# Two recurrent layers of a fused model: output copies on ScalarE, adds to X and one weighting on GpSimd

## The reference, cut to what matters

```
v = x @ value_w.T ;  r = sigmoid(x @ recep_w.T)
wkv_t = (e1_t * aa_t + e2_t * v_t) / (e1_t * bb_t + e2_t + 1e-6)
aa_{t+1} = e1b_t * aa_t + e2b_t * v_t
return (r * wkv) @ out_w.T
```

```
multiplier = sqrt(max(1 - a*a, 1e-7)) ;  normed_x = x * gate_x * multiplier
p_prefix = max(shifted cumprod(a), 1e-7)
S = cumsum(normed_x / p_prefix) ;  h = p_prefix * S ;  return h
```

## Time and profile before

| | us |
|---|---|
| median of 3 runs | 3088.95 |
| lowest and highest run | 3085.35 and 3089.32 |
| the profiled execution | 3088.85 |
| its span, first to last instruction | 3087.0 |
| window of the first recurrent loop, 207.5 to 252.4 | 44.90 |
| window of the second layer's last loop, 1893 to 1926.6 | 33.60 |

### The profile page before, as it was taken

The page is one execution under the profiler, slowest core; times in us unless marked ns, Lnnn a source line. Parts: engine busy times, 40 slices in busy tenths (PEclk is TensorE's granted clock), DMA queues, the critical chain, the costliest instruction groups (busy, mean ns, idle before and its releaser), DMA issues. The chain is left out here.

```text
span 3087.0 us, 102826 instructions
## 1 busy us (share of the span) xinstructions
PE 2499.1 (81%) x30020; PEld 1971.3 (64%) x30021; DVE 2154.2 (70%) x7789; ACT 1872.6 (61%) x5990; POOL 1776.9 (58%) x1942
## 2 busy tenths in 40 slices
PE   4964799489999879888999983489669999979571
PEld 2843687367777678766777761477547777758561
DVE  5978422478888868727888887632279999979525
ACT  3841444379999723347999975144358888847320
POOL 1832477367777664025777762057547777749271
PEclk9985899799999989889999996589889999989685
DMA  2002455311111030003333320135534544500132
GB/s 103 3 1 99 128 154 153 98 45 41 39 39 39 27 130 0 0 1 76 79 79 79 81 46 0 66 117 153 147 82 116 115 118 114 116 5 3 57 106 67
DMA packets 195910, 225.58 MB, mean 73 GB/s; under 512 B 24899, under 2 KB 166211, under 8 KB 194724
## 3 DMA queue, kind: packets, MB, share of 16 engines
q1 hardware_dynamic: 183076, 197.57, 24.3%
q0 software_dynamic: 12672, 25.98, 3.1%
HBM read 201.69 MB, written 21.76 MB: 72 GB/s over the span
## 5 line engine op out<-in xcount | busy, mean ns | idle before, releaser
L1803 POOL TENSOR_TENSOR sx<-sx,rs 128x1028 f32<-128x1028 f32 x384 | 731.3, 1904 | 280.4 <-DVE rs L1951 280.2
L1896 ACT ACTIVATE sx<-sx,nm 128x257 f32<-128x257 f32 x1536 | 771.1, 506 | 115.8 <-DVE nm L1939 115.8
L1939 DVE CUSTOM_DVE_ANT_0 sx<-bank,rows 128x257 f32<-128x257 f32 x1024 | 411.1, 421 | 50.8 <-PE bank L1886 48.5
L1606 ACT ACTIVATE hT<-bank,B 128x128 f32<-128x128 f32 x714 | 205.7, 367 | 279.6 <-PE bank L1574 277.8
L350 POOL TENSOR_TENSOR rstd<-var,nhalf 128x8 f32<-128x8 f32 x48 | 79.1, 1648 | 414.0 <-DVE var L381 414.0
L1896 ACT ACTIVATION_READ_ACCUMULATOR sx<-sx,nm 128x1 f32 x1536 | 290.9, 189 | 0.0
L1886 PE MATMUL bank<-kT,qb 32*128 32x257 f32 x3072 | 278.6, 428 | 0.0
L1958 DVE COPY pt<-bank 128x512 f32<-128x512 f32 x384 | 263.8, 687 | 2.0 <-PE bank L1821 1.7
L1821 PE MATMUL bank<-C,sx 128*128 128x128 f32 x1536 | 251.6, 286 | 2.8 <-POOL sx L1803 2.7
L1840 PEld LDWEIGHTS bank<-W,ct 128*128 128x128 f32 x1536 | 219.5, 192 | 52.1 <-DVE nm L1939 18.1
L1870 PE MATMUL bank<-pt,vs 128*32 128x128 f32 x6144 | 245.6, 277 | 4.7 <-ACT pt L1905 4.6
(11 more groups left out here) (391 smaller groups left out, 5629.4 us busy)
## 6 DMA issues: line engine op xcount, KB each, us to landing
ct<-in_ctxT SPq DMA_DIRECT2D x384, 128.5 KB
W<-in_L_w SPq DMA_DIRECT2D x159, 256.0 KB
rows<-rows_x SPq DMA_DIRECT2D x256, 128.5 KB
keep<-rows_keep SPq DMA_DIRECT2D x128, 128.5 KB
yg<-copy_outs SPq DMA_DIRECT2D x40, 256.0 KB
token_rows<-XN SPq DMA_DIRECT2D x24, 256.0 KB, 2.3
W<-in_L_w SPq DMA_DIRECT2D x1, 6144.0 KB, 16.9
W<-in_L_w SPq DMA_DIRECT2D x39, 128.0 KB
```

The costliest lines, as they stand in the source:

```text
L1803: pool.tensor_tensor(sx[:, j, :, 0:KEYS], sx[:, j, :, 0:KEYS], rs[:, j, :].unsqueeze(2).to_broadcast([P, 4, KEYS]), ALU.mult).then_inc(p_r ...
L1896: ins = act.activation(sx[:, j, h, 0:KEYS], sx[:, j, h, 0:KEYS], ACT.Exp, bias=nm[:, j, h:h + 1], scale=-1.0, accum_out=sm[:, j, h:h + 1])
L1939: dve.tensor_tensor_reduce(sx[:, j, h, 0:KEYS], B[h][:, 0:KEYS], add, -1.0, 3.0e38, ALU.add, ALU.min, nm[:, j, h:h + 1]).then_inc(s_summed ...
```

## The change

In `rwkv`, GpSimd weights the values of group k into `y` as soon as the matmuls of group k-2 have read that buffer, and VectorE waits for it (`v_weighted`) ahead of the sum. In both layers ScalarE copies the bank of each of the first seven groups into a new buffer `ob` (two halves of 4 x 128 columns), GpSimd adds `ob` to X, and TensorE waits for the copy instead of for the add. The last group's bank is still added to X by VectorE. Sums and products stay the same.

```diff
 # rwkv
+                ob = sb2("ob", [P, 2, GT, P])
-                y_psum, x_added = sig("y_psum", 8), sig("x_added", 8)
+                y_psum, v_weighted = sig("y_psum", 8), sig("v_weighted", 8)
+                out_copied, x_pooled = sig("out_copied", GROUPS - 1), sig("x_pooled", GROUPS - 1)
...
 # VectorE, for each group, behind the scan and the weighting of aa
-                            dve.wait_ge(*y_psum(g - 1))
-                            st_.link(dve.tensor_tensor(y[:, q], vg, per_batch(RW[:, 1, :], S), ALU.mult))
+                        dve.wait_ge(*v_weighted(g + 1))
                         st_.link(dve.tensor_tensor(y[:, q], y[:, q], aa[:], ALU.add))
...
-                            dve.wait_ge(*y_psum(g + 1))
-                            xg = X[:, g * GT:(g + 1) * GT, :]
-                            dve.tensor_tensor(xg, xg, B[g % 2][:].rearrange("p (t d) -> p t d", t=GT), ALU.add).then_inc(x_added.sem, 1)
+                    g = GROUPS - 1
+                    dve.wait_ge(*y_psum(g + 1))
+                    xg = X[:, g * GT:(g + 1) * GT, :]
+                    dve.tensor_tensor(xg, xg, B[g % 2][:].rearrange("p (t d) -> p t d", t=GT), ALU.add)
...
+                @block.gpsimd
+                def _(pool):
                     for k in range(GROUPS + 1):
+                        if k < GROUPS:
+                            vg = VT[:, k * GW:(k + 1) * GW].rearrange("p (b s) -> p b s", s=S)
+                            pool.wait_ge(*y_psum(k - 1))
+                            pool.tensor_tensor(y[:, k % 2], vg, per_batch(RW[:, 1, :], S), ALU.mult).then_inc(v_weighted.sem, 1)
+                        g = k - 2
                         if g >= 0:
+                            pool.wait_ge(*out_copied(g + 1))
                             xg = X[:, g * GT:(g + 1) * GT, :]
+                            pool.tensor_tensor(xg, xg, ob[:, g % 2], ALU.add).then_inc(x_pooled.sem, 1)
+
+                @block.scalar
+                def _(act):
+                    for g in range(GROUPS - 1):
+                        act.wait_ge(*y_psum(g + 1))
+                        act.wait_ge(*x_pooled(g - 1))
+                        act.copy(ob[:, g % 2].rearrange("p t d -> p (t d)"), B[g % 2][:]).then_inc(out_copied.sem, 1)
...
 # TensorE, in both layers
-                        pe.wait_ge(*x_added(g - 1))
+                        pe.wait_ge(*out_copied(g - 1))
...
 # rglru, GpSimd, behind its eight products
+                    for g in range(GROUPS - 1):
+                        pool.wait_ge(*out_copied(g + 1))
+                        xg = X[:, g * GT:(g + 1) * GT, :]
+                        pool.tensor_tensor(xg, xg, ob[:, g % 2], ALU.add).then_inc(x_pooled.sem, 1)
...
 # rglru, ScalarE
+                    def copy_out(g):
+                        act.wait_ge(*x_pooled(g - 1))
+                        act.copy(ob[:, g % 2].rearrange("p t d -> p (t d)"), B[g % 2][:]).then_inc(out_copied.sem, 1)
...
                         act.activation(p[:, g % 2, :], CS[:, tok(g)], ACT.Exp, scale=lru[:, 0:1]).then_inc(p_ready.sem, 1)
+                        if g >= 2:
+                            copy_out(g - 2)
+                    act.wait_ge(*y_psum(GROUPS - 1))
+                    copy_out(GROUPS - 2)
```

More of the change, by code:

```diff
@@ L72 @@
            "up_psum", "gelu_ready", "down_psum", "copied", "logits", "stage_ready",
-           "c_turned", "c_ready", "x_turned", "xT_ready", "u_psum", "u_ready", "uT_psum", "h_ready", "yb_psum", "yb_ready", "copy_ready", "scan_ready", "a_done", "b_done", "c_done", "d_done", "e_done", "hot_ready", "hot_used", "step_ready", "hi_ready", "at_ready", "at_turned"]
+           "c_turned", "c_ready", "x_turned", "xT_ready", "out_copied", "v_weighted", "x_pooled", "u_psum", "u_ready", "uT_psum", "h_ready", "yb_psum", "yb_ready", "copy_ready", "scan_ready", "a_done", "b_done", "c_done", "d_done", "e_done", "hot_ready", "hot_used", "step_ready", "hi_ready", "at_ready", "at_turned"]
 class Signal:
@@ L682, in _ @@
                     flat = "p b s -> p (b s)"
-                    for k in range(GROUPS + 1):
[L684 to L690, removed]
-                            dve.wait_ge(*y_psum(g - 1))
-                            st_.link(dve.tensor_tensor(y[:, q], vg, per_batch(RW[:, 1, :], S), ALU.mult))
[L694 to L697, removed]
@@ new lines, in _ @@
+                    for g in range(GROUPS):
+                        q = g % 2
+                        vg = VT[:, g * GW:(g + 1) * GW].rearrange("p (b s) -> p b s", s=S)
+                        st_.link(dve.tensor_tensor(ub[:, :, 1:S], vg[:, :, 0:S - 1], per_batch(recur[:, 0:S - 1], S - 1), ALU.mult))
+                        st_.link(dve.tensor_tensor_scan(aa[:].rearrange(flat), decay[:].rearrange(flat), ub[:].rearrange(flat),
+                                                        0.0, ALU.mult, ALU.add))
+                        st_.link(dve.tensor_tensor(aa[:], aa[:], per_batch(RW[:, 0, :], S), ALU.mult))
+                        dve.wait_ge(*v_weighted(g + 1))
+                        st_.link(dve.tensor_tensor(y[:, q], y[:, q], aa[:], ALU.add))
+                        dve.tensor_tensor(y[:, q], y[:, q], RT[:, g * GW:(g + 1) * GW].rearrange("p (b s) -> p b s", s=S), ALU.mult)\
+                            .then_inc(scan_ready.sem, 1)
@@ new lines, in _ @@
+                    g = GROUPS - 1
+                    dve.wait_ge(*y_psum(g + 1))
+                    xg = X[:, g * GT:(g + 1) * GT, :]
+                    dve.tensor_tensor(xg, xg, B[g % 2][:].rearrange("p (t d) -> p t d", t=GT), ALU.add)
+                    st_.close()
+                @block.gpsimd
+                def _(pool):
+                    for k in range(GROUPS + 1):
+                        if k < GROUPS:
[3 more added lines that the diff above has]
+                        g = k - 2
@@ L698, in _ @@
                         if g >= 0:
-                            dve.wait_ge(*y_psum(g + 1))
+                            pool.wait_ge(*out_copied(g + 1))
                             xg = X[:, g * GT:(g + 1) * GT, :]
-                            dve.tensor_tensor(xg, xg, B[g % 2][:].rearrange("p (t d) -> p t d", t=GT), ALU.add).then_inc(x_added.sem, 1)
-                    st_.close()
+                            pool.tensor_tensor(xg, xg, ob[:, g % 2], ALU.add).then_inc(x_pooled.sem, 1)
+                @block.scalar
@@ L727, in rglru @@
                 gx_ready, cs_ready, p_ready = sig("q_built", 8), sig("centred", 8), sig("probs_ready", 8)
-                scan_ready, y_psum, x_added = sig("scan_ready", 8), sig("y_psum", 8), sig("x_added", 8)
+                ob = sb2("ob", [P, 2, GT, P])
+                scan_ready, y_psum = sig("scan_ready", 8), sig("y_psum", 8)
+                out_copied, x_pooled = sig("out_copied", GROUPS - 1), sig("x_pooled", GROUPS - 1)
                 block = c2.enter_context(nc.Block())
@@ new lines, in _ @@
+                    for g in range(GROUPS):
+                        q = g % 2
+                        dve.wait_ge(*gx_ready(g + 1))
+                        dve.wait_ge(*root_ready(g + 1))
+                        st_.link(dve.tensor_tensor(GX[:, tok(g)], GX[:, tok(g)], A2[:, tok(g)], ALU.mult))
+                        dve.wait_ge(*p_ready(g + 1))
+                        st_.link(dve.scalar_tensor_tensor(out=GX[:, tok(g)], in0=ip[:, q, :], scalar=1e7, in1=GX[:, tok(g)],
+                                                          op0=ALU.min, op1=ALU.mult))
+                        st_.link(dve.tensor_tensor_scan(A2[:, tok(g)], keeps, GX[:, tok(g)], 0.0, ALU.mult, ALU.add))
+                        dve.scalar_tensor_tensor(out=p[:, q, :], in0=p[:, q, :], scalar=1e-7, in1=A2[:, tok(g)],
+                                                 op0=ALU.max, op1=ALU.mult).then_inc(scan_ready.sem, 1)
@@ L787, in _ @@
+                    dve.wait_ge(*y_psum(GROUPS))
+                    xg = X[:, (GROUPS - 1) * GT:GROUPS * GT, :]
+                    dve.tensor_tensor(xg, xg, B[(GROUPS - 1) % 2][:].rearrange("p (t d) -> p t d", t=GT), ALU.add)
                     st_.close()
```

## The result

The changed kernel is slower: 3100.38 us median of 7 runs (3098.14 to 3106.22) against 3088.08 (3085.35 to 3089.32), a ratio of 1.0043 with a 95% interval of 1.0031 to 1.0055, that is 13.3 us (9.6 to 17). Forecast were +8.2 us and a range of 3086 to 3104. Its profiled execution took 3098.33 us, span 3096.5. Both loops went as forecast, to a few tenths of a microsecond; what came on top, some 5 us by the runs, lies in stages that the change does not touch.

A forecast was written before the change was run, and what follows sets the result against it. VectorE's chain was taken to bound both loops: 12.9 us come off and 22 GpSimd turns at 0.96 us put on 21.1, so +8.2 on 3088.85 gives 3097 us; range 3086 to 3104.

The forecast's parts named there:

- The chain on VectorE: Both recurrent loops: VectorE's instructions form one chain, so any microsecond taken off or put on moves the end.
- What is taken off: Both loops' VectorE chain: eight weightings, 5.8 us, and six adds per layer, 3.5 us each; together 12.9 us.
- ScalarE, TensorE and GpSimd's own time at nothing: Both loops: ScalarE's 0.58 us copies, TensorE's wait for them and GpSimd's own instruction time are hidden, costing nothing.
- The price of a turn: Both loops: each of GpSimd's 22 instructions is put between two of VectorE's, costing 0.96 us, 21.1 us in all.
- the lower bound: Price from below: 0.88 us per turn, 0.65 for weightings if of the 1.047 us kind; 17.5 us in all.
- The loops' sum: Both loops: 21.1 - 12.9 = +8.2 us, the first layer +5.1 and the second +3.2.
- The shift should pass to the end of the kernel undiminished: After both loops: stages end at barriers, so the loops' shift of +8.2 us reaches the kernel's end in full.
- the forecast's own bounds: Whole time by the price's bounds, 17.5 to 23.5 us: +4.6 to +10.6, or 3093.5 to 3099.5 us; chance 0.68.
- rival 3: Both loops: VectorE's instruction loses GpSimd's whole 1.27 us each time; 3104 us, chance 0.05.
- Rival 1: Both loops: GpSimd and VectorE do not hinder each other, so 12.9 us are gained; 3076 us, chance 0.10.
- rival 2: Both loops: VectorE keeps its turn and GpSimd waits; only weightings cost, 10.2 us, net -2.7, about 3086; chance 0.17.

The follow-up runs named there:

- e5: Changed kernel with GpSimd's 22 instructions replaced by constant fills that read nothing, all waits kept; loops 35.57 and 31.35 us, one run.
- e7: Kernel before plus ScalarE's seven first-layer bank copies into an unread buffer, VectorE and TensorE waiting for them; ratio 1.0012 (1.0003 to 1.0021).
- e8: Kernel before, unchanged, timed against itself as a control; ratio 1.0002 (0.9993 to 1.0012).
- e3: Against the kernel before: TensorE adds X into the bank by an identity product, ScalarE copies it back, VectorE still weights; ratio 0.9983 (0.9974 to 0.9992).

## Why the prediction was right, and where it was short

**The chain on VectorE** decides both loops: right. Every edit moved the loops by what it took off this chain or put on it.

**What is taken off**, 12.9 us: right; 9.39 + 3.60 = 13.0 in e5.

**ScalarE, TensorE and GpSimd's own time at nothing**: right in the loops. For the copies e7 shows it; in the changed kernel's trace VectorE waits nowhere in the two loops for GpSimd, and its waits for ScalarE, 2.7 and 0.5 us at the second loop's start, are as long as before.

**The price of a turn**, 0.96 us: right, 0.94 and 0.96. The kind of GpSimd instruction that is shorter by 0.23 us costs 0.76, where the lower bound had put it at 0.65.

**The loops' sum**, +8.2: 4.75 + 3.14 = +7.9.

**"The shift should pass to the end of the kernel undiminished"** is the step that was short. It was undiminished, but not unaccompanied: with the first layer's edit came some 4 us in the two cross-attention stages behind it. I had looked for things that could absorb a shift and not asked whether another program could run the same code at another speed. That is the difference between +8.2 and the 12 to 13 us measured. The median, 3100.4, lies above the forecast's own bounds, 3093.5 to 3099.5; that it lies within the stated range is luck, since the range reached up to 3104 for the sake of rival 3, whose mechanism is not the one that added these 4 us.

**Rival 1** (no hindrance, 3076) and **rival 2** (VectorE keeps its turn, 3086) are refuted by the stretched products in the profile after, and rival 2 also by VectorE's having no wait for GpSimd there. **Rival 3** (the whole 1.27 us lost each time) comes near the measured total, but by accident: the loops show 0.94 to 0.96, with 1.07 in the position it named, GpSimd ahead by 0.06 us. The Trainium skill's Advanced Engine Details and Errata, "Mode Summary", which names two-port instructions alone and by which the time would have been rival 1's, does not cover these products: they are held all the same, 1.63 us for 0.69.

## What to carry to other kernels

Before moving work from VectorE to GpSimd, look at what is left on VectorE: where that takes two tensors from SBUF, each GpSimd instruction that reads SBUF was put in between here, and the work moved was paid on the same chain, with 0.95 us for steps of 0.59 and 0.725. Fills in its place, or giving the work to TensorE and ScalarE, had no such price. And the length of these two loops, read from marks that both traces have, was reproducible to 0.02 us where whole runs of one kernel differ by 4 us or more, so effects of a few microseconds are best read in the stage that is edited, with the whole time as a check on what else moved. Not every stage is so steady: the two cross-attention stages differ by 1.3 us in sum between before and e8, which are one program.

## What the runs showed of the hardware that was not expected

With a product on TensorE put in front of the next group's, that group's products took 1.16 us for 2.08 in five of eight groups of e3, with the granted clock at 1.00 and not at 0.50 in the last of them; so work added to an engine with time to spare can come with a shorter tail, though not in every group. A GpSimd sum of a tile with itself takes 1.04 us where two different tiles take 1.27. And some 4 us in two stages came with edits that add waits of another engine to an earlier stage, as a few matmuls that are late in each turn of a loop, by a cause that these runs do not show.

VectorE's steps with two SBUF tensors are not the only ones that GpSimd holds up. In the stage ahead of the second loop, in the kernel before, VectorE clips A2, one SBUF tensor, while GpSimd's products run; nanoseconds min/median/max:

```profile
L768 DVE TENSOR_SCALAR A<-A x8: 397/907/1422, 1873.3 to 1890.8; 128x512 f32<-128x512 f32 x8
```

The four clips that begin while GpSimd's products run take 1.42 us, the four behind them 0.40.
